# The attention and feed-forward part of a decoder layer in another instruction order: w2 accumulated unit by unit behind w1

## The reference, cut to what matters

```python
x = _layernorm(x + mamba(x))                       # ends in y @ W_out + b_out
q, k, v = x @ wq.T + bq, ctx @ wk.T + bk, ctx @ wv.T + bv      # heads of 32
scores = where(mask == 0, -1e9, q @ k.T / sqrt(32)); probs = softmax(scores)
x = _layernorm(x + (probs @ v) @ wo.T + bo)
hidden = x @ W1 + b1                               # 2048 columns
imag = w_imag * sin(theta + 0.1 * hidden)
act = relu(hidden + (cos(theta) * w_real + sin(theta) * w_imag) * imag * 0.1)
x = _layernorm(x + act @ W2 + b2)
```

## Time and profile before

| | |
|---|---|
| median of 3 runs | 3524.76 us (3520.2 to 3528.44) |
| the profiled execution's own time | 3536.19 us |
| its span, first to last instruction | 3534.3 us |
| first phase, about | the first 1995 us of the span |
| mean granted TensorE clock over the span | 0.914 |
| busy over the span | PE 2971.4 us, DVE 2813.4 us, ACT 1938.4 us, POOL 2109.9 us |

### The profile page before, as it was taken

How to read it: one execution, slowest core, us unless ns; L and a number is a source line. 1 busy time by engine, 2 the same in 40 slices (tenths; PEclk the granted TensorE clock), 3 DMA queues, 4 the chain that set the end, 5 groups by cost and what they waited for, 6 DMA issues and landing times. The chain is left out here.

```text
span 3534.3 us, 49312 instructions
## 1 busy us (share of the span) xinstructions
PE 2971.4 (84%) x18868; PEld 1341.0 (38%) x18868; DVE 2813.4 (80%) x2954; ACT 1938.4 (55%) x3475; POOL 2109.9 (60%) x1117
## 2 busy tenths in 40 slices
PE   5978788788788787887888579998888888888897
PEld 2222222222222222221222155555555566655564
DVE  3999999999999999999999856666666666666664
ACT  4776666667666766676664444444444444444443
POOL 3788988888989889898897422222232233332221
PEclk8999999999999999998996579999999999999999
DMA  3111121111111111111113310000000000000000
GB/s 139 60 38 58 37 66 42 37 54 51 45 57 45 57 45 39 57 47 50 51 40 102 115 60 25 25 25 25 25 19 25 19 13 24 25 25 25 25 8 13
DMA packets 92544, 153.63 MB, mean 43 GB/s; under 512 B 12001, under 2 KB 29025, under 8 KB 91874
## 3 DMA queue, kind: packets, MB, share of 16 engines
q1 hardware_dynamic: 92386, 151.54, 13.5%
HBM read 92.79 MB, written 58.72 MB: 43 GB/s over the span
## 5 line engine op out<-in xcount | busy, mean ns | idle before, releaser
L713 POOL TENSOR_TENSOR h<-h,c_rep 128x1024 f32<-128x1024 f32 x512 | 1199.6, 2357 | 251.0 <-ACT carry L527 250.9
L643 DVE TENSOR_TENSOR_SCAN h<-r_ps,carry,h 128x512 f32<-128x512 f32 x768 | 941.7, 1269 | 27.3 <-ACT r_ps L521 27.1
L521 ACT ACTIVATE r_ps<-r_ps,decay 128x512 f32<-128x512 f32 x1024 | 632.6, 657 | 330.2 <-PE r_ps L295 329.9
L630 DVE TENSOR_TENSOR h<-u_ps,b_rep 128x1024 f32<-128x1024 f32 x512 | 617.9, 1207 | 32.1 <-PE u_ps L306 31.1
L1462 POOL TENSOR_TENSOR units<-units 128x512 f32<-128x512 f32 x128 | 162.4, 1269 | 460.1 <-DVE units L1319 460.1
L306 PE MATMUL u_ps<-dtu,spread 32*128 32x512 f16 x2048 | 334.2, 406 | 109.9 <-DVE h L630 108.8
L295 PE MATMUL r_ps<-dt,spread 32*128 32x512 f16 x2048 | 331.6, 403 | 75.9 <-DVE h L643 63.5
L318 PE MATMUL y_ps<-h,gather 128*32 128x512 f32 x2048 | 302.7, 660 | 89.8 <-POOL h L713 88.7
L643 DVE TENSOR_TENSOR_SCAN h<-r_ps,zero,h 128x512 f32<-128x512 f32 x256 | 314.0, 1270 | 12.1 <-ACT r_ps L521 12.1
L40 PE MATMUL fps<-x,region 128*128 128x256 f16 x1024 | 292.8, 286 | 24.6 <-ACT units L1140 22.2
L42 PE MATMUL fps<-x,region 128*128 128x256 f16 x1024 | 292.3, 285 | 0.0
(11 more groups left out here) (219 smaller groups left out, 6036.7 us busy)
## 6 DMA issues: line engine op xcount, KB each, us to landing
u_t_dram<-u SPq DMA_DIRECT2D x16, 1024.0 KB, 4.8
z_t_dram<-zs SPq DMA_DIRECT2D x32, 512.0 KB, 2.9
uz<-u_t_dram SPq DMA_DIRECT2D x64, 256.0 KB, 3.8
uz<-z_t_dram SPq DMA_DIRECT2D x64, 256.0 KB, 4.4
y_t_dram<-y SPq DMA_DIRECT2D x64, 256.0 KB, 2.3
y_t<-y_t_dram SPq DMA_DIRECT2D x15, 1024.0 KB, 6.1
x_in<-dram_x SPq DMA_DIRECT2D x16, 512.0 KB, 3.5
result<-x SPq DMA_DIRECT2D x16, 512.0 KB, 3.1
```

The source lines that it names most:

```text
L521: nc.scalar.activation(bank, bank, ACT.Exp, scale=decay[:, col:col + 1]).then_inc(s_da, 1)
L630: nc.vector.tensor_tensor(h[:, g % H_GROUPS, o:o + 2, :], u_ps[:, :, :], b_rep[:, c % 2:c % 2 + 1, :].broadcast_to([P, 2, TS]), ALU.mult). ...
L643: nc.vector.tensor_tensor_scan(row, r_ps[:, 2 * (pair % 2) + o, :], row, start, ALU.mult, ALU.add)\
L713: nc.gpsimd.tensor_tensor(rows, rows, c_rep[:, c % 2:c % 2 + 1, :].broadcast_to([P, 2, TS]), ALU.mult)\
```

## The change

PE's order in a step is new. `second(b, n)` now adds one unit for both token tiles, and runs about three units behind `hidden`; the pieces of the front stand between. The out projection and the output projection go into the two banks of `sps` instead of `nat`, and the second tile's out projection is cut in two halves around the transposes of x2. `nat` is left to w2. The values are taken out of `tr` one token tile at a time. On DVE the `fraction` subtraction joins the rounding (it was on POOL), and the mask is applied by one minimum with a cap, where it was a product and then a sum with `fill` over both tiles. The norm of w2's result (`finish_output`) and the store of the output move into the next step, ahead of that step's second out-projection residual. ACT's and DVE's orders are rewritten: for units 4 to 7 every step of a unit stands before the next unit, with the softmax of the front between them.

```diff
@@ semaphores, queues
-MASKED = 1.0e9
+MASKED = -1.0e9
+KEPT = 3.0e38
@@ SP
-                    sp.wait_ge(s_keep, c * 2)
+                    sp.wait_ge(s_cap, c * 2)
                     load_mask(c, batch)
+                if back and not (isinstance(c, int) and c == 1):
+                    store_out(c - 2)
...
-                if back:
-                    sp.wait_ge(s_x["w2"], c * NT)
-                    load(a["out"]...[:, bass.ds((c - 1) * NT, NT), :], x3[:, :, :], s_out)
+                if back and not front:
+                    store_out(c - 1)
@@ PE
-            def second(b, t, n0, n1):
-                for n in range(n0, n1):
-                    pe.wait_ge(s_actl, b * NU + n + 1)
-                    natural(act16, w_2, NF, t, 2 * n, 2 * n + 2, s_nat["w2"])
+            def second(b, n, tiles=range(NT)):
+                pe.wait_ge(s_actl, b * NU + n + 1)
+                for t in tiles:
+                    if n == 0:
+                        pe.wait_ge(s_r["w2"], b * NT)
+                    natural(nat[:, t, :], act16, w_2, NF, t, 2 * n, 2 * n + 2, s_nat["w2"])
+            def out_projection(c, t, k0, k1, back):
+                if k0 == 0:
+                    pe.wait_ge(s_yl, c + 1)
+                    if back:
+                        pe.wait_ge(s_r["wo"], (c - 1) * NT + t + 1)
+                natural(sps[:, t, :], y16, w_out, NJ, t, k0, k1, s_nat["outproj"])
```

```diff
@@ ACT (the part of a step from the queries on; relu(b, 3) to values_high are in program order)
+                    relu(b, 3)
...y_high(c + 1)
+                    hid_out(b, 4)
+                    sine(b, 4)
+                    relu(b, 4)
+                    hid_out(b, 5)
+                    exps(c, 0)
+                    sine(b, 5)
+                    relu(b, 5)
+                    hid_out(b, 6)
+                    sine(b, 6)
+                    exps(c, 1)
+                    relu(b, 6)
+                    hid_out(b, 7)
+                    sine(b, 7)
+                    probs_out(c, 0, (0, 1))
+                    relu(b, 7)
+                    probs_out(c, 0, (2, 3))
+                    values_high(c, 0)
+                    probs_out(c, 1, (0, 1, 2, 3))
+                    values_high(c, 1)
@@ ACT (start of a step)
+                    deviation("wo", 1, b)
                     nc.scalar.activation(x2_16[:, 0, :, :], tr[:, :, :], ACT.Copy).then_inc(s_x2t, 1)
+                    deviation("w2", 2, b - 1)
                     deviation("outproj", 0, c)
+                    hid_out(b, 0), hid_out(b, 1), sine(b, 0), hid_out(b, 2)
                     nc.scalar.activation(xa16[:, 0, :, :], tr[:, :, :], ACT.Copy).then_inc(s_x1t, 1)
+                    sine(b, 1), relu(b, 0), hid_out(b, 3), sine(b, 2), relu(b, 1), sine(b, 3), relu(b, 2)
@@ DVE
-            def whole_turns(b, n):
+            def fraction(b, n):
                 dve.wait_ge(s_h, b * NU + n + 1)
                 nc.vector.tensor_scalar(whole[:, n % 2, :, :], arg[:, n % 3, :, :], ROUND, ROUND, ALU.add, ALU.subtract)\
                     .then_inc(s_wh, 1)
+                dve.wait_ge(s_wh, b * NU + n + 1)
+                nc.vector.tensor_tensor(arg[:, n % 3, :, :], arg[:, n % 3, :, :], whole[:, n % 2, :, :], ALU.subtract)\
+                    .then_inc(s_fr, 1)
@@ masked
-                                            keep[:, t:t + 1, :].broadcast_to([P, HU, CTX]), ALU.mult).then_inc(s_sc, 1)
-            def softmax_a(c, t):
-                nc.vector.tensor_tensor(pr[:, t, :, :], pr[:, t, :, :], fill[:, t:t + 1, :].broadcast_to([P, HEADS, CTX]),
-                                        ALU.add).then_inc(s_sma, 1)
+                                            cap[:, t:t + 1, :].broadcast_to([P, HU, CTX]), ALU.min).then_inc(s_sc, 1)
+            def row_maximum(c, t): ...      # the reduction that was in softmax_a
+            def less_maximum(c, t): ...     # the subtraction that was in softmax_a
@@ DVE, one step with front and back, after (a comma is program order)
+ statistics + normalize wo(b), residual outproj tile 0, low of x2, finish_output(b - 1),
+ residual outproj tile 1, statistics + normalize outproj, fraction 0, fraction 1, mix 0, low of x1,
+ fraction 2, mix 1, act_low 0, fraction 3, mix 2, act_low 1, mix 3, act_low 2, act_low 3,
+ mask, masked(0, 0-1), masked(0, 2-3), fraction 4, row_maximum 0, masked(1, 0-1), less_maximum 0,
+ mix 4, act_low 4, masked(1, 2-3), fraction 5, row_maximum 1, softmax_b 0, less_maximum 1,
+ mix 5, act_low 5, fraction 6, softmax_b 1, mix 6, act_low 6, fraction 7, mix 7, act_low 7,
+ values_low 0, values_low 1, residual w2, residual wo
@@ POOL
-            def fraction(b, n):
-                pool.wait_ge(s_wh, b * NU + n + 1)
-                nc.gpsimd.tensor_tensor(arg[:, n % 3, :, :], arg[:, n % 3, :, :], whole[:, n % 2, :, :], ALU.subtract)\
-                    .then_inc(s_fr, 1)
```

More of the change, by code:

```diff
@@ L1051, in front_back @@
                 if back:
-                    hidden(b, 6)
+                    second(b, 1)
                 if front:
@@ L1069, in front_back @@
                 if back:
-                    second(b, 0, 3, 5)
+                    hidden(b, 5)
                 if front:
@@ L1177, in front_back @@
                 if back:
-                    for n in range(4):
-                        hid_out(b, n)
-                        if n >= 1:
-                            sine(b, n - 1)
-                        if n >= 2:
-                            relu(b, n - 2)
+                    hid_out(b, 0)
+                    hid_out(b, 1)
+                    sine(b, 0)
+                    hid_out(b, 2)
                 if front:
@@ L1190, in front_back @@
                 if back:
-                    for n in range(4, 6):
-                        hid_out(b, n)
-                        sine(b, n - 1)
-                        relu(b, n - 2)
+                    sine(b, 1)
+                    relu(b, 0)
+                    hid_out(b, 3)
+                    sine(b, 2)
+                    relu(b, 1)
+                    sine(b, 3)
+                    relu(b, 2)
                 if front:
@@ L1288, in _, with residual @@
             weights_low(3)
-            def residual(n, c, x, xb_sem, into, tiles=range(NT)):
+            def residual(n, c, out, x, xb_sem, into, tiles=range(NT)):
                 for t in tiles:
@@ L1396, in front_back @@
                 if back:
-                    for n in range(4):
-                        unit(b, n)
+                    fraction(b, 0)
+                    fraction(b, 1)
+                    mix(b, 0)
                 if front:
                     low_of_tr(xa16, s_x1t, c + 1, s_x1l)
-                if back:
-                    for n in range(4, 7):
-                        unit(b, n)
                 if not back:
@@ L1481, in front_back @@
                     add_bias(x2, 2, s_xb["wo"])
-                if back:
-                    for n in range(5):
-                        fraction(b, n)
                 if front:
@@ L1487, in front_back @@
                     add_bias(x1, 1, s_xb["outproj"])
-                if back:
-                    for n in range(5, 8):
-                        fraction(b, n)
                 if front:
```

240 lines of the change are left out of this document (135 added, 105 removed).

## The result

The changed kernel takes 3604.31 us (median of 4, 3599.38 to 3608.7), the kernel before 3526.6 us (median of 4 runs, 3520.2 to 3528.54): ratio 1.0223, 95% interval 1.0204 to 1.0243. It is slower by 78 us; 3625 had been forecast, in a range of 3540 to 3675.

A forecast was written before the change was run, and what follows sets the result against it. PE was taken as near its limit (82.86 of 92.16 us busy, 9.30 idle). 15 x (99.4 - 92.15) = 108.8, less 8.5, gave +100 us on the median 3524.8: 3625 us, range 3540 to 3675.

The forecast's parts named there:

- Start of a period: Output projection to hidden 2: PE idles 2.0 us for hid_out 0, which waits behind finish_output and the deviation.
- First w2 unit: Before second 0: PE idles 3.4 us for act_low 0, then loses 1.7 us to the low clock.
- The middle chain: ACT and DVE, units 4 to 7 with softmax: probs_out at 85.2, PE idle 11.9 us before the third probs_t quarter.
- Waits for POOL: DVE and POOL instructions reading two SBUF tensors wait for each other; probs holds up mix 5 and 6, 4.3 us together.
- The end: Behind 85.2: 9.8 us of PE work plus 4.3 us lost to the low clock, period 99.3.
- the 99.4 of the sum: Predicted period in us, small waits included, against 92.15 before; 15 x the difference is 108.8 us.
- Outside the 15: First and last step, outside the 15 full periods: gains of 2.5 and 6 us, together -8.5 us.
- (1): Rival: same ACT and DVE chain without the POOL waits, 95.1 us a period, 3560 us; 3535 to 3590 had chance 0.21.
- (2): Rival: the middle chain hides behind PE, period 83.4 us, 3385 us; any time below 3517 had chance 0.11.
- (3): Rival: ACT table switches cost 1.28 us more at three places, 3.8 a period, 3682 us; chance 0.13 shared with (4).
- (4): Rival: low clock at two more places, 1.7 us each, period 102.8, 3676 us; chance 0.13 shared with (3).
- (5): Rival: order makes no difference because PE's work is the same; chance 0.05, shared with a 92.4 us period case.

The follow-up runs named there:

- Experiment 5a: Changed kernel with finish_output, its deviation and the store moved later in the step, to the end of unit 3: 3574.73 us.
- Experiment 1: Changed kernel with ACT's four copies of tile 0's transposed probabilities moved right behind the second exponential, ahead of relu 6: 3568.09 us.
- experiments 1 and 4: The second of these: changed kernel, PE's order kept, ACT and DVE orders rewritten from unit 4 to overlap units, POOL's next-x bias ahead of y_low: 3489.21 us.
- experiment 5c: Changed kernel with probs moved from POOL to DVE, behind act_low 5 and 6, and POOL's bias on the next x ahead of y_low: 3574.34 us.
- experiment 5: Three separate edits of the changed kernel: finish_output later, 3574.73 us; second 0 behind the queries, 3542.41; probs on DVE, next-x bias earlier, 3574.34.
- experiment 6: Changed kernel, units overlapped, finish_output, second 0 and x1 bias later: 3443.86 us; then also probs on DVE, both biases after act_low 7, sine 6 earlier: 3343.74.

## Why the prediction was right, and where its sizes were off

Times within a period are counted, as in the prediction, from the start of the output projection, here 2746.10 us; the next starts at 2844.50.

**Start of a period.** PE idles for `hidden` 2: 2.0 predicted, 1.91 measured. Experiment 5a, which moves only `finish_output`, takes it away; its cause is shown.

**First w2 unit.** 3.4 us predicted, 3.79 measured. The step was right, but a term was missing in it: `mix` 0, which the walk does not name, took 3.01 us instead of 0.88, because POOL's bias on x1 (2773.80, 2.36) ran beside it. The prediction lists no wait for this bias. Most of the delay was covered: the low part of x1 behind it started at 2776.36, and ACT's high part, which it needs as well, had ended at 2775.76, so 0.6 us of it reached `act_low` 0. The low clock lasted for 5.1 us of PE's work (2780.13 to 2785.2), 2.5 us lost where 1.7 was put.

**The middle chain.** Predicted: PE idle 11.9 us, the third quarter of `probs_t` at 85.2. Measured: 10.94 us, and the third quarter at 2832.47, which is 86.4. Experiment 1 shows that ACT's program order is the last link, and experiments 1 and 4 that the links before it are the serial steps of units 4 to 7: overlapped, they leave 2.47 us.

**Waits for POOL.** `mix` 5 and 6 met `probs` as walked (2.86 and 2.78); 4.3 us was put on them, experiment 5c took 3.5 off that idle time. The wait of `act_low` 6 (1.4 us) was not walked as such; 0.5 us of `fraction` 7 behind the bias stood for it. The subtraction that the trace of before did not show took 0.69, the upper bound, where 0.65 was taken. The prediction had the holding between instructions that read two SBUF tensors. The rounding, a TENSOR_SCALAR that reads one, is held as well: 1.43 us in experiment 5, 2.47 in experiment 6, where it takes 0.41 to 0.43 otherwise. The Trainium skill, "SBUF — State Buffer", section "SBUF: two separate sides", says that GpSimd and VectorE share an SBUF port pair and that one holds the other off; the rows with 2.86, 2.47 and 3.32 us agree.

**The end, the mis-sized term.** After 11.9 us of idle the walk gave PE 8.59 us at 0.50, 4.3 lost. The windows above show 3.57 us at 0.50 after PE's restart; steps of 0.1 us have the low clock from 2826.15 to 2836.35, so PE did 3.9 us of work in it and 1.9 were lost. For 6.3 us of the low clock PE did nothing. The tail from the third quarter to the next output projection is 12.0 us (2844.50 - 2832.47) and not the 14.1 of the walk: 2.1 too much, with 2.4 for the clock and 0.3 the other way. The chain itself came 1.2 later than walked, so this period of 98.4 is 0.9 short of 99.3. Over the mean of 97.83, the 99.4 of the sum is 1.57 too long: 15 x 1.57 = 23.6 us too much.

**Outside the 15.** Predicted -8.5. The second phase, counted from its first load of x, grew from 1538.5 to 1618.1 us, by 79.6, of which the periods are 15 x 5.68 = 85.2: -5.6. So 2.9 us of gain were missing here, and 23.6 - 2.9 is the whole overshoot of 20.7 us (3625 - 3604.31): two errors that partly cancel, which is luck as far as the total goes. The span grew by only 63.4, since the first phase, whose code is the same, was 16.1 us longer in the profiled execution of before (its own time 3536.19 lies 9.6 above the median of 3526.6).

**The rivals.** (1), the chain without the POOL waits, is what experiment 5c tried: `mix` 5 and 6 fall to their quiet length, but the time is 3574, not 3560; the wait that this edit made before `second` 0 is told there. (2), the chain hidden behind PE, did not come in the changed kernel; it is what the kernels of experiment 6 come to with further moves, 79.82 a period where I had 83.4. (3), dearer table switches: six loads of 1283 ns and a start 1.30 us after, so nothing beyond the row. The drain that the prediction quotes from the Trainium skill, "ScalarE: Activation LUTs", section "What ACT_TABLE_LOAD costs", is not seen here. (Three drains of that size make 4.1 us and not 3.8, so the estimate by them should have been 3687 us.) (4), low clock at more places: the changed kernel has it at the two places named and at no other in this period. (5), no difference: excluded by 5.68 us a period.

## What to carry to other kernels

Two pipelines interleaved on one PE need their ACT and DVE steps interleaved too: written one whole unit after another, the serial chain of units 4 to 7 with the softmax between left PE idle for 10.94 us a period. With the other places it hid 148 us of real gains, so try the parts of a large reordering on the old order first. Before POOL is given or relieved of anything, write its instructions beside DVE's by start time: the mask's minimum gained 94 us with only 2.8 us a period of removed work, and by its rows the rest came from `less_maximum` starting before `y_low`; moving the bias on x1 gained 30 us and removed nothing. A moved POOL instruction can also cost: the bias on the next x, beside `fraction` 2, cost 1.0 us a period before `second` 0. A first consumer placed right behind its producer's chain (`second` 0) is cheap to move behind a piece that needs nothing from it: 62 us for one moved line.

## What the runs showed of the hardware

The low clock begins inside an idle time, and the work that it slows does not grow with the idle time: 8.6 us of work at 0.50 after 4.81 us of idle before the change, 5.1 after 3.79 and 3.9 after 10.94 in the changed kernel. For the first and the last of these the whole low stretch is equally long, about 10.2 us: 2698.75 to 2708.95 in the kernel before, where PE restarted 1.7 us into it, and 2826.15 to 2836.35 in the changed one, where PE restarted 6.3 us into it. What PE lost was the part that came after its restart. Rows just inside the two stretches, the kernel before and then the changed one:

```profile
2698.80:2708.90 10.10, 8.49 (x30) 4.72 (x31) 8.44 (x11) 1.23 (x1) 3.31 (x1) 0.50 0.00 0
```
```profile
2826.20:2836.30 10.10, 3.83 (x13) 2.48 (x14) 5.82 (x7) 6.76 (x12) 3.37 (x2) 0.50 0.00 0
```

The length is not always this one: around the 3.79 us of idle the low clock ran from 2778.35 to 2785.15, and what sets it stays open.

DVE and POOL hold each other in both directions, and a TENSOR_SCALAR that reads one tensor is held too (2.47 and 1.43 us instead of 0.43). Of two DVE instructions in a row the second can be the one that waits: POOL, waiting since 2812.41, got in between `less_maximum` 1 and `mix` 5.
